# Places of their own for the steps of a five-thread order, and the last states kept by sums of one element

## The reference, cut to what matters

```python
x = x + attention_block(layernorm(x))   # LN, 16 heads of 16, sliding window of 128, softmax, w_o,
                                        # LN, gelu(h @ w1 + b1) @ w2 + b2 with 1024 hidden columns
x = x + rwkv_channel_mix(layernorm(x))  # sigmoid(xr @ W_r) * (relu(xk @ W_k)**2 @ W_v), xr and xk mix a row with the row before
x = x + mamba(layernorm(x))             # below
x = x + expert(layernorm(x))            # of 8 experts the one that the mean row of the batch element picks:
                                        # relu(x @ W1[e] + b1[e]) @ W2[e] + b2[e], 1024 hidden columns

# mamba, 512 channels, 16 states each
xp, z = split(x @ in_w.T)
xc = silu(causal_conv4(xp))
dt, B, C = split(xc @ x_proj.T)
delta = softplus(dt @ dt_w.T + dt_b)
h[t] = exp(delta[t] * A) * h[t-1] + delta[t] * B[t] * xc[t]      # for each channel and state
y = sum_over_states(h * C) + D * xc
out = (y * silu(z)) @ out_w.T
```

## Time and profile before

| | |
|---|---|
| median of 3 runs | 3521.13 us (3517.15 to 3521.82) |
| the profiled execution's own time | 3517.29 us |
| its span, first to last instruction | 3515.4 us |
| PE busy | 2997.9 us, 85% |
| POOL busy | 2646.4 us, 75% |
| DVE busy | 2605.4 us, 74% |
| ACT busy | 2392.8 us, 68% |
| mean granted TensorE clock | 0.919 |
| read from and written to HBM | 388.79 MB and 84.93 MB |

### The profile page before, as it was taken

How to read it: one execution, slowest core, us unless ns; L and a number is a source line. 1 busy time by engine, 2 the same in 40 slices (tenths; PEclk the granted TensorE clock), 3 DMA queues, 4 the chain that set the end, 5 groups by cost and what they waited for, 6 DMA issues and landing times.

```text
span 3515.4 us, 54603 instructions
## 1 busy us (share of the span) xinstructions
PE 2997.9 (85%) x17328; PEld 1868.9 (53%) x17328; DVE 2605.4 (74%) x5644; ACT 2392.8 (68%) x5299; POOL 2646.4 (75%) x1590
## 2 busy tenths in 40 slices
PE   5888888888988989899898889989898998987567
PEld 3555455554655656465564646556464665654236
DVE  3257968797787867778687877779677786878880
ACT  5577768686776867677686767767676776864531
POOL 1118889888788888877887888888888778887680
PEclk9999989899999999999899999989999898998778
DMA  2013434445443443543445353344535434454541
GB/s 76 13 65 122 138 128 135 148 128 172 129 150 132 145 171 117 186 128 125 149 150 172 110 193 125 124 154 139 180 114 188 127 128 155 138 188 150 171 132 38
DMA packets 285966, 477.31 MB, mean 136 GB/s; under 512 B 38450, under 2 KB 93362, under 8 KB 285682
## 3 DMA queue, kind: packets, MB, share of 16 engines
q1 hardware_dynamic: 285682, 473.83, 40.9%
HBM read 388.79 MB, written 84.93 MB: 135 GB/s over the span
## 4 chain that ended last, share of the span: by engine, by line
PE 52%; POOL 15%; issue 11%; DVE 10%; ACT 9%; DMA 2%; SPq 1%; ACTq 0%; POOLq 0%; DVEq 0%
PE bank L482 14%; PE bank L490 7%; PE bank L605 6%; POOL h_rows L1503 6%; POOL h_rows L1513 6%; PE bank L741 5%; PE bank L727 5%; PE bank L680 4%; PE bank L527 4%; PE bank L515 3%; DVE h_rows L1279 3%; PE bank L543 2%; ACT prob L796 2%; DMA u_rows<-u_dram 1%; ACT bank L967 1%
## 5 line engine op out<-in xcount | busy, mean ns | idle before, releaser
L1513 POOL TENSOR_TENSOR h_rows<-h_rows,c_rows 128x1024 f32<-128x1024 f32 x480 | 1131.0, 2360 | 327.7 <-DVE state L1286 207.0
L1503 POOL TENSOR_TENSOR h_rows<-u_rows,b_rows 128x1024 f32<-128x1024 f32 x512 | 1199.1, 2361 | 10.7 <-DMA b_rows<-bc_dram 8.3
L967 ACT ACTIVATE bank<-d_rows,a_rep 128x512 f32<-128x512 f32 x1024 | 692.1, 687 | 201.4 <-DVE v_pad L1089 55.7
L1279 DVE TENSOR_TENSOR_SCAN h_rows<-bank,state,h_rows 128x512 f32<-128x512 f32 x480 | 600.4, 1270 | 87.8 <-ACT bank L967 86.6
L1279 DVE TENSOR_TENSOR_SCAN h_rows<-bank,h_rows 128x512 f32<-128x512 f32 x480 | 575.4, 1210 | 65.4 <-ACT bank L967 63.9
L796 ACT ACTIVATE prob<-prob,neg_max 128x256 f32<-128x256 f32 x1024 | 509.4, 504 | 25.9 <-DVE neg_max L1062 25.9
L527 PE MATMUL bank<-ident,prob 128*128 128x128 f32 x2048 | 334.0, 289 | 109.0 <-ACT prob L796 84.1
L527 PEld LDWEIGHTS bank<-ident,prob 128*128 128x128 f32 x2048 | 239.5, 146 | 314.1 <-issue 264.4
L1062 DVE CUSTOM_DVE_ANT_0 prob<-bank,bands 128x256 f32<-128x256 f32 x896 | 334.4, 415 | 93.3 <-PE bank L515 68.4
L680 PE MATMUL bank<-h_rows,sum_n 128*32 128x512 f32 x2048 | 307.9, 677 | 92.9 <-POOL h_rows L1513 79.9
L515 PE MATMUL bank<-kT,q_own 32*128 32x256 f32 x2048 | 301.1, 413 | 17.9 <-DVE h_rows L1279 7.3
(11 more groups left out here) (164 smaller groups left out, 5025.3 us busy)
## 6 DMA issues: line engine op xcount, KB each, us to landing
u_rows<-u_dram SPq DMA_DIRECT2D x256, 256.0 KB, 3.9
d_rows<-delta_dram SPq DMA_DIRECT2D x256, 256.0 KB, 3.1
b_rows<-bc_dram SPq DMA_DIRECT2D x256, 256.0 KB, 3.1
c_rows<-bc_dram SPq DMA_DIRECT2D x256, 256.0 KB, 3.1
w<-in_W SPq DMA_DIRECT2D x28, 1024.0 KB, 7.1
zs_dram<-region_b SPq DMA_DIRECT2D x64, 256.0 KB, 2.0
xc_dram<-region_b SPq DMA_DIRECT2D x64, 256.0 KB, 2.6
u_dram<-region_b SPq DMA_DIRECT2D x64, 256.0 KB, 2.3
```

The costliest lines, as they stand in the source:

```text
L967: e.activation(banks[at.bank][:, :], d_rows[:, c, :], ACT.Exp, scale=a_rep[:, k:k + 1]).then_inc(filled[at.bank], 1)
L1279: e.tensor_tensor_scan(rows, banks[at.bank][:, :], rows, start, ALU.mult, ALU.add).then_inc(drained[at.bank], 1)
L1503: e.tensor_tensor(half_of(i, b, half), u_rows[:, 2 * half:2 * half + 2, :], twice(b_rows[:, b % 2, :]), ALU.mult).then_inc(bx_ready.sem, 1)
L1513: e.tensor_tensor(rows, rows, twice(c_rows[:, b % 2, :]), ALU.mult).then_inc(hc_ready.sem, 1)
```

## The change

`COSTS` and the lag, begin and end of `THREADS` go. A table `PLACES` gives each step of each stage a place of its own, in ten-thousandths of a period counted from the group's own zero; a step's place is `10000 * i + place`. How steps are then taken (order of places, chains ahead, idle banks) stays, as do the stages, their steps and what a step does. Beside it the copy of the last states becomes a sum over an axis of one element, with the same two words read and written.

```diff
-SCAN_PERIOD = 136
-COSTS = {
-    "head": [2.45] * 6,
-    "attention": [1.81] * 2 + [0.8] * (ATT0 - 2 + 18) + [1] * 54 + [1.5] + [1.57] * 4,
-    "mlp": [1.5] * 2 + [1] * 8 + [1.31] * 8 + [4] + [1.04] * 8 + [2.5] * 3,
-    "rwkv": [1.5] * 5 + [1] * 11 + [1.6] + [2.5] * 3,
-    "middle": [1.68] * 2 + [1] * 8 + [1.15] * 8 + [1] * 11,
-    "scan": [1] * SCAN_STEPS,
-    "back": [2.26] + [1] * 4 + [2.06] * 3 + [1] * 2,
-    "route": [1] * 3,
-    "fetch": [1],
-    "expert": [1] * 12 + [0.95] * 13,
+PLACES = {
+    "head": (
+        -231, 487, 704, 726, 960, 1319,
+    ),
+    "attention": (
+        1398, 1483, 1555, 1661, 1661, 1836, 1970, 1970, 1970, 2011, 2328, 2331, 2334, 2419, 2691, 2806, 2806, 2806,
...
+        7908, 7908, 8016, 8057, 8135, 8564, 8573, 8680, 8733, 8974, 9141, 9259, 9455, 9806, 9806, 9995, 10130, 10295,
+        10392,
+    ),
+    "mlp": (
+        8694, 9613, 9801, 10414, 10513, 10705, 11050, 11050, 11059, 11096, 11242, 11356, 11389, 11389, 11389, 11469,
+        11477, 12040, 12332, 12382, 12748, 12874, 12885, 12950, 12987, 13188, 13392, 13500, 13610, 13956,
+    ),
+    "rwkv": (
+        14127, 14181, 14274, 14274, 14293, 14673, 14777, 14924, 14934, 15076, 15164, 15185, 15460, 15639, 15639,
+        15706, 16258, 16258, 16407, 16612,
+    ),
+    "middle": (
+        16755, 16894, 17127, 17177, 17346, 17379, 17518, 17688, 17750, 17832, 17910, 18105, 18110, 18489, 18567,
+        18567, 18732, 18734, 19070, 19128, 19261, 19470, 19506, 19506, 19506, 19619, 19771, 20180, 20535,
+    ),
+    "scan": (
+        19744, 19889, 19889, 20934, 20950, 20978, 20990, 20990, 20990, 20990, 20990, 21053, 21053, 21254, 21446,
...
+        23663, 23872, 24239, 24239, 24272, 24327, 24327, 24327, 24382, 24508, 24714, 24714, 24714, 24743, 24845,
...
+        25804, 26070, 26298, 26382, 26545, 26545, 26546, 26640, 26765, 26765, 26766, 26766, 26766, 26822, 26890,
+        26904, 26904, 26904, 27268, 27286, 27286, 27353, 27354, 27438, 27492, 27641, 27906, 27906, 27922, 27922,
...
+        30354, 30458, 30512, 30512, 30929, 31054, 31257, 31308, 31503, 31558,
+    ),
...
+    "expert": (
+        44524, 44862, 45177, 45622, 45775, 46078, 46274, 46366, 46489, 46658, 46662, 46896, 47255, 47266, 47680,
+        47811, 47936, 48899, 48900, 49150, 49654, 49660, 49704, 49950, 49984,
+    ),
 }
 THREADS = (
-    (("head", "attention"), 0, 0.0, 1.0),
-    (("mlp", "rwkv", "middle"), 1, 0.0, 1.0),
-    (("scan",), 2, 0.041, 0.041 + SCAN_STEPS / SCAN_PERIOD),
-    (("back",), 3, 0.16, 0.35),
-    (("route",), 3, 0.407, 0.437),
-    (("fetch",), 4, 0.437, 0.447),
-    (("expert",), 4, 0.467, 0.979),
+    ("head", "attention",),
+    ("mlp", "rwkv", "middle",),
+    ("scan",),
...
 )
@@ schedule
-    for thread, (stages, lag, begin, end) in enumerate(THREADS):
-        total = sum(sum(COSTS[stage]) for stage in stages)
+    for thread, stages in enumerate(THREADS):
...
-                for step, cost in enumerate(COSTS[stage]):
-                    chain.append((i + lag + begin + (end - begin) * spent / total, thread, stage, which, step))
-                    spent += cost
+                for step, place in enumerate(PLACES[stage]):
+                    chain.append((10000 * i + place, thread, stage, which, step))
@@ keep_states in dve_scan
-                    e.tensor_copy(state[:, k:k + 2], half_of(i, b, half)[:, :, G - 1]).then_inc(state_ready.sem, 1)
+                    e.tensor_reduce(state[:, k:k + 2], half_of(i, b, half)[:, :, G - 1:G], AX.X, ALU.add).then_inc(state_ready.sem, 1)
```

More of the change, by code:

```diff
@@ L47 @@
 SCAN_STEPS = SCAN0 + 8 * (QUADS - 1) + GATE_AT + 1
-SCAN_PERIOD = 136
-COSTS = {
-    "head": [2.45] * 6,
-    "attention": [1.81] * 2 + [0.8] * (ATT0 - 2 + 18) + [1] * 54 + [1.5] + [1.57] * 4,
-    "mlp": [1.5] * 2 + [1] * 8 + [1.31] * 8 + [4] + [1.04] * 8 + [2.5] * 3,
-    "rwkv": [1.5] * 5 + [1] * 11 + [1.6] + [2.5] * 3,
-    "middle": [1.68] * 2 + [1] * 8 + [1.15] * 8 + [1] * 11,
-    "scan": [1] * SCAN_STEPS,
-    "back": [2.26] + [1] * 4 + [2.06] * 3 + [1] * 2,
-    "route": [1] * 3,
-    "fetch": [1],
-    "expert": [1] * 12 + [0.95] * 13,
+PLACES = {
[3 more added lines that the diff above has]
+    "attention": (
[6 rows of a table added]
+    ),
[12 more added lines that the diff above has]
+    "scan": (
[10 rows of a table added]
+    ),
+    "back": (
+        30891, 32003, 32013, 32137, 32285, 32364, 32452, 33159, 33209, 33372,
+    ),
+    "route": (
+        32159, 34023, 34044,
+    ),
+    "fetch": (
+        43940,
+    ),
+    "expert": (
+        44524, 44862, 45177, 45622, 45775, 46078, 46274, 46366, 46489, 46658, 46662, 46896, 47255, 47266, 47680,
+        47811, 47936, 48899, 48900, 49150, 49654, 49660, 49704, 49950, 49984,
+    ),
 }
 THREADS = (
-    (("head", "attention"), 0, 0.0, 1.0),
-    (("mlp", "rwkv", "middle"), 1, 0.0, 1.0),
-    (("scan",), 2, 0.041, 0.041 + SCAN_STEPS / SCAN_PERIOD),
-    (("back",), 3, 0.16, 0.35),
-    (("route",), 3, 0.407, 0.437),
-    (("fetch",), 4, 0.437, 0.447),
-    (("expert",), 4, 0.467, 0.979),
+    ("head", "attention",),
+    ("mlp", "rwkv", "middle",),
+    ("scan",),
+    ("back",),
+    ("route",),
+    ("fetch",),
+    ("expert",),
 )
@@ L127, in schedule @@
     chains = {}
-    for thread, (stages, lag, begin, end) in enumerate(THREADS):
-        total = sum(sum(COSTS[stage]) for stage in stages)
+    for thread, stages in enumerate(THREADS):
         for i in range(2 * batches):
-            chain, spent = [], 0.0
+            chain = []
             for stage in stages:
@@ L142, in schedule @@
     begins, ends = {}, {}
-    for stage in COSTS:
+    for stage in PLACES:
         for shared in (False, True):
@@ L149, in earlier @@
     def earlier(thread, i):
-        out = [] if THREADS[thread][0] == ("scan",) else [(thread, i - 1)]
+        out = [] if THREADS[thread] == ("scan",) else [(thread, i - 1)]
         if thread:
-            out.append((thread - 1, i | 1 if THREADS[thread][0] == ("fetch",) else i))
+            out.append((thread - 1, i | 1 if THREADS[thread] == ("fetch",) else i))
         return out
```

## The result

The changed kernel takes 3228.93 us (median of 4 runs, 3228.1 to 3229.66) against 3521.48 us before (median of 4 runs, three of them those of the table before): a ratio of 0.9165, 95% interval 0.915 to 0.918, so 8.35% or 292.5 us faster. Forecast were 3434 us, with 3360 as the lower end: the way was right, the size was a third of what came.

What follows compares the result with a forecast made beforehand. PE in fixed order was taken as the bound. Terms sum to -4.2 us a period, -63 us over 15 groups, -87 with the copies: 3434 us forecast from 3521, with 3360 to 3530 as the range for 8 in 10.

Steps and rivals of the forecast that it cites:

- The bound: PE, taking steps in fixed order, sets the pace; about 22 us of each 206.9 us period are holes.
- The copy, 24 us: Copy of last states waits for POOL, a reduce does not; even periods 3.0 us longer, so eight even groups give 24.
- The long hole, -4.0 us: PE's wait between product o and t2, `mlp`'s first transposes, for rows zb: 8.8 us shrinks to 4.8 a period.
- The clock behind it, -1.7 us: PE's slow clock behind the long hole costs 3.5 us a period; the shorter hole halves it, gaining 1.7.
- t2 to h0, t3 to rk0, +1.5 us: Less work between these PE steps: losses of 0.5 us before the first hidden product and 1.0 before rk0, per period.
- The rest, unchanged between -4 and +4: PE's other holes, 13 us a period, taken as unchanged, bounds -4 and +4 us a period.
- The POOL clumps: Rival: POOL's big products crowd three twentieths of a period, overrun 14 us, PE's sums wait: 3584 us, 14%.
- The reload of the weights: Next `mlp`'s weights, asked for 11.4 us ahead instead of 14.6, just hold, with half a microsecond in hand.
- Holes close wholly: Rival: the 8.8 us hole and the slow clock behind it go wholly, 186 us with the copies: 3335 us, 14%.
- The signs: If right: sum 0.14 to 0.17 us, even and odd periods equal, zb wait about 5 us, periods 201 to 203.

Runs made afterwards that it cites:

- e2: Kernel before with its old order exactly, but the sum over one element in place of the copy of the last states: 3520.13 us, ratio 0.9991.
- e1: Changed kernel with its new places but the old copy of the last states instead of the sum: 3287.02 us, ratio 0.9329.
- e11: Changed kernel with four softplus steps of `middle` put behind the product o again: 3335.33 us, ratio 0.9457.
- e12: Changed kernel with w_1 reloaded early and the expert stage's last product moved from ahead of o to behind it: 3183.42 us, ratio 0.903.
- e10: Changed kernel with every new place rounded to a whole hundred (2 us): 3605.79 us, ratio 1.023.
- e3: Changed kernel with the scan's old places, new places for all other stages, and the sum: 3520.29 us, ratio 1.0.
- e4: Changed kernel with old places for all stages but the scan, which keeps its new ones, and the sum: 3574.7 us, ratio 1.0149.

## Why the prediction was wrong, by its own steps

*The bound.* Right: PE in a fixed order sets the pace, and what an order can give is its holes, 22 us a period. PE went from 52% to 70% of the chain.

*The copy, 24 us.* Wrong in its reason. By itself the edit is worth 1 us (e2), under the new order 58 us (e1 against the changed kernel). The mechanism was right: with the copy DVE stands behind POOL's product, the sum (101 to 158 ns in 240) never does, as the Trainium skill has it ("SBUF — State Buffer", Who interferes with whom). What failed is reading its price from even against odd periods: with the copies gone, e2's even periods stayed at 208.4 us. The copies' waits lay beside others in the old order; in the new one they reach PE, as e1's waits for DVE show.

*The long hole, -4.0 us.* Right: 8.8 to 4.4 us in the mean, t2 10.05 us after o for 10.5; e11 shows that the softplus steps' place is worth 106 us, with what it opens beside. One reading in it was off without effect: two POOL products, not three, ran between o's start and the power, and the power waited 2.21 us for the statistics, not for POOL.

*The clock behind it, -1.7 us.* A term that was mis-sized: 6.6 us a period. I gave the clock back only at the one long hole. There the slow time fell from 13.6 to 9.0 us in the mean, worth half of it, 2.3 us, within my bounds; but the whole period's slow time fell from 26.0 to 12.4 us. The other 12.4 us a period stood for the most part around the holes for the exponentials, as the earlier trace rows show behind one of 3.1 us and this window of the kernel before shows behind two of 1.0 and 0.7 us; 3.4 of the 12.4 us are left:

```profile
2571.00:2575.00 4.00, 4.00 (x47) 2.15 (x45) 3.07 (x11) 2.13 (x6) 4.00 (x2) 0.68 0.01 2
```

The six holes of that period at other places, 0.8 to 1.9 us long, have no slow time behind them. e12, with no hole over 2.5 us, has 2.6 us of slow time a period left.

*t2 to h0, t3 to rk0, +1.5 us.* Neither loss came. Of the first wait, 1.5 us by my count, 0.7 us a period came (7.4 us in ten), less than the 1.1 us for POOL that stood there before; rk0 waits for nothing in the list.

*The rest, unchanged between -4 and +4.* This is the step that failed: all holes but the long one went from 13.8 to 4.6 us a period, 9.3 us, about 139 us over the kernel. Of these, 6.3 us are the order's alone, since with the copy kept (e1) 7.5 are left, and 3.0 are the sum's, where the whole edit had been priced at 1.6. I weighed the PE work between the ends of fifteen dependences, found eight better and five worse by a few microseconds, and took that for no change. The count was too coarse: in e10 no place moves by more than 50, 1 us, so the PE work between two ends hardly changes, and yet the holes grow by 17 us a period. What is left to decide whether a wait ends in time is what stands ahead of it on DVE, ACT and POOL. I had done that count, engine by engine, for one dependence only; there it came out within half a microsecond. That it would have priced the others as well is likely and not shown.

*The rivals.* The POOL clumps cost nothing: the sums waited 0.9 us in ten periods, places being no times. They do decide where attention's places are the old ones. The reload of the weights just held, 2.4 us in ten periods, as counted. "Holes close wholly" (3335, 14%) was the nearest, and it too had the rest's holes unchanged.

*The signs.* The sum lay between 0.101 and 0.158 us, below the 0.14 to 0.17 that I gave; even and odd periods are within 0.8 us of one length and zb's wait is near 5 us, as said; the periods are 186.5 us long and not 201 to 203.

What stays open: why the order has this gain in terms of single steps. e3 to e10 show that it is joint and fine, not which of the few hundred neighbour relations of a period carry it.

## What to carry to other kernels

Where engines run fixed lists from several threads, price a new order by following each wait through the instructions ahead of it on every engine that it passes, not by the cover on the bounding engine; a smoothed or rounded version of a finely placed order is another order. A stall on an engine off the path may be worth nothing now and 2% after the order is tightened, so try such edits again once it is. And count a hole of PE with the slow clock behind it: breaking up the one hole of 4.4 us took only 1.1 us of idle time a period away and gave back another 3.5 us of clock.

## What the runs showed of the hardware that was not expected

A copy of two floats can stand through more than one product of POOL. Before, the longest took 2.32 us and ended with the product that was running. With the new order (e1) the longest took 3.86 us: it began at 1121.60 us, inside a POOL product that ended at 1122.99, stood through the whole next one, from 1122.90 to 1125.28, and ended at 1125.46.

PE's slow time does not follow the sum of its idle time. The granted clock was 0.96 to 0.97 in periods with one hole of 4.2 to 4.5 us and 0.98 to 1.00 in those of e12, whose longest hole is 2.5 us, though PE is idle 8.9 and 7.8 us a period. With the scan's new places alone (e4) PE is idle 27.3 us a period and 20.9 us are at the slow level; in the kernel before it is idle less, 22.7 us, and 26.0 us are slow.
